# The second norm of a graph and LSTM kernel without back transposes: row factors through DRAM, two scaling passes on VectorE, a rewritten passage and end

## The reference, cut to what matters

```
h = item_feat @ W_item.T + b_item                 # 10000 x 128
b = layernorm(x) @ W_user.T + b_user
x1 = x + relu(adj @ h + b)
z = layernorm(x1) @ W_ih.T + b_ih + b_hh          # input of the LSTM, the "second norm"
i, f, g, o per step: c = sig(f) c + sig(i) tanh(g); hs = sig(o) tanh(c)
g = argmax(hs @ W_lin.T + b_lin)                  # 0 or 1 per row
w = g * hs; inc = cumsum(w); prefix = inc - w; suffix = inc[-1] - inc
out = x1 + 2 hs + prefix * fw_att + suffix * bw_att
```

## Time and profile before

| what | value |
|---|---|
| median of 3 runs | 1447.24 us |
| profiled execution | 1444.94 us, of which the span 1443.1 us |
| granted TensorE clock over the span | 0.993 |
| busy: TensorE, VectorE, ScalarE, GpSimd | 1412.8, 1242.8, 1067.8, 214.5 us |
| HBM read, written | 422.42 MB, 10.28 MB |

### The profile page before, as it was taken

One profiled execution on the slowest core, in us unless ns is written; L12 is line 12 of the kernel. 1 busy time (PEld: TensorE's weight loads), 2 busy tenths in 40 slices (PEclk: granted clock), 3 DMA queues, 4 the chain that ended last, 5 costly groups with the idle time before them and its releaser, 6 DMA issues.

```text
span 1443.1 us, 26187 instructions
## 1 busy us (share of the span) xinstructions
PE 1412.8 (98%) x7478; PEld 1214.0 (84%) x7478; DVE 1242.8 (86%) x2052; ACT 1067.8 (74%) x1502; POOL 214.5 (15%) x193
## 2 busy tenths in 40 slices
PE   8999999999999999999999999999999899999994
PEld 7878888888888888888888888888888799999993
DVE  7998998998998999999989989989989666676667
ACT  6677777777877877877877877777777576556662
POOL 0000010010001001001001001000000132027775
PEclk9999999999999999999999999999999999999997
DMA  9999999999999999999999999999999203000003
GB/s 374 360 331 357 403 364 370 407 360 362 404 365 364 407 357 364 407 355 377 396 358 387 385 352 401 378 347 403 373 362 400 87 0 142 0 2 0 1 0 143
DMA packets 134877, 433.16 MB, mean 300 GB/s; under 512 B 18683, under 2 KB 35900, under 8 KB 134718
## 3 DMA queue, kind: packets, MB, share of 16 engines
q1 hardware_dynamic: 127776, 426.43, 78.0%
q10 hardware_dynamic: 7070, 6.34, 1.6%
HBM read 422.42 MB, written 10.28 MB: 300 GB/s over the span
## 4 chain that ended last, share of the span: by engine, by line
PE 91%; DVE 3%; issue 2%; POOL 2%; DMA 1%; ACT 0%; POOLq 0%; DVEq 0%; SPq 0%; ACTq 0%
PE psG L842 24%; PE psG L843 24%; PE psG L844 24%; PE psZ L965 8%; PE psZ L951 2%; PE psZ L953 2%; PE psZ L955 2%; PE psG L863 1%; PE psT L810 1%; PE psI L890 1%; DVE a_lo L1130 1%; POOL own L526 1%; PE psZ L971 1%; DMA raw<-in_adj_main 1%; POOL own L529 1%
## 5 line engine op out<-in xcount | busy, mean ns | idle before, releaser
L634 ACT ACTIVATE a_hi<-raw 128x1000 fp32r<-128x1000 f32 (+1 forms) x800 | 821.8, 1031 | 244.8 <-PE psG L844 208.4
L1130 DVE TENSOR_TENSOR a_lo<-raw,a_hi 128x1000 fp32r<-128x1000 f32 (+1 forms) x800 | 911.0, 1170 | 74.5 <-ACT a_hi L634 55.2
L842 PE MATMUL psG<-a_hi,item_hi 128*128 128x500 f32 x1560 | 620.5, 398 | 2.1 <-DVE a_lo L1130 1.1
L843 PE MATMUL psG<-a_lo,item_hi 128*128 128x500 f32 x1560 | 606.0, 388 | 0.0
L844 PE MATMUL psG<-a_hi,item_lo 128*128 128x500 f32 x1560 | 604.7, 388 | 0.0
L842 PEld LDWEIGHTS psG<-a_hi,item_hi 128*128 128x128 f32 x1560 | 293.5, 188 | 66.9 <-issue 5.6
L844 PEld LDWEIGHTS psG<-a_hi,item_lo 128*128 128x128 f32 x1560 | 293.2, 188 | 59.4
L843 PEld LDWEIGHTS psG<-a_lo,item_hi 128*128 128x128 f32 x1560 | 293.6, 188 | 58.6 <-issue 4.4
L452 POOL TENSOR_TENSOR rstd<-var,minus_half 125x4 f32<-125x4 f32 x40 | 76.1, 1902 | 1019.5 <-DVE var L1106 1019.5
L965 PE MATMUL psZ<-hist,wh 128*128 (+1 forms) x1264 | 167.8, 276 | 1.2 <-DVE hist L1304 1.1
L965 PEld LDWEIGHTS psZ<-hist,wh 128*128 128x128 f32 x1264 | 154.9, 192 | 1.7 <-issue 1.6
(11 more groups left out here) (174 smaller groups left out, 769.9 us busy)
## 6 DMA issues: line engine op xcount, KB each, us to landing
raw<-in_adj_main SPq DMA_DIRECT2D x760, 500.0 KB, 6.5
raw<-in_adj_main SPq DMA_DIRECT2D x40, 250.0 KB, 4.5
sq<-rstd_copy ACTq DMA_DIRECT2D x20, 250.0 KB, 7.1
x_copy<-xb SPq DMA_DIRECT2D x20, 250.0 KB, 7.1
u<-x_copy SPq DMA_DIRECT2D x1, 5000.0 KB, 14.4
out<-u SPq DMA_DIRECT2D x25, 200.0 KB, 2.4
u<-in_itemT SPq DMA_DIRECT2D x9, 512.0 KB, 10.1
xb<-in_xT SPq DMA_DIRECT2D x18, 250.0 KB, 5.9
```

What stands on the lines that cost most here:

```text
L634: nc.scalar.activation(a_hi[:, s % CUT, 0:n], raw[:, r % RAW, at:at + n], ACT.Copy)\
L842: pe.matmul(bank, w_hi, hi, start=(c == 0), stop=False)
L843: pe.matmul(bank, w_hi, lo, start=False, stop=False)
L1130: last = dve.tensor_tensor(a_lo[:, s % CUT, 0:m], raw[:, r % RAW, at:at + m], a_hi[:, s % CUT, 0:m].bitcast(f32), ALU.subtract)
```

## The change

**Second norm.** `normalise` and `to_columns` are gone. `rstd` and `shift_rows` become the two halves of one tile `row_terms`. ScalarE stores it in DRAM (`send_terms`, r = 8) and reads each half back to all partitions (`spread_terms`, r = 12) into `factors` (which is `sq`) and `rl` (which is `un_bb`). VectorE then multiplies and adds (`apply_rstd`, r = 16; `apply_shift`, r = 17) over 128 x 500, into `normed`. `row_scale` moves from r = 6 to 7, `out_u` from 10 to 18, and reads `normed` in SBUF instead of `psV`. `add_relu` writes a tile of its own, `x1b`, so the load of the next x waits for `x1_ready` alone.

**Passage.** TensorE runs 8 products of `ident` with itself whose result nobody reads (`KEEP_WARM`), then step 1's recurrent part for group a before the back transposes; its step for group b comes after the split inputs of step 2. ScalarE and VectorE take up the cell of step 1 earlier, and `input_hi(1)` moves ahead of step 0's second group.

**End.** GpSimd adds hist and x1 of its last pair before it waits for the gate. ScalarE copies the last two rows of x1 to a tile without strides (`x1_last`) during the LSTM. TensorE adds row L - 2 up before the last logits, and the totals before row L - 1. `total` is computed before the second `last_y`, and ScalarE writes the shift twice, to PSUM for VectorE and to SBUF for GpSimd. There are 13 outputs of 400, 800 or 1000 columns (GpSimd still has 80 chains of 250), and the check stands behind all of them.

```
+OUT_ENDS = (10, 20, 30, 40, 60, 80, 105, 130, 155, 180, 205, 230, K)
+POOL_OUTS = (3, 5, 8, 11)
-AT = dict(... scale2=6, norm2=7, back2=8, out2=10,
+AT = dict(... scale2=7, send2=8, spread2=12, apply2=16, shift2=17, out2=18,
...
-            def normalise(count):
-                act.wait_ge(ln_scale, count)
-                for s in range(SUB):
-                    last = nc.scalar.activation(normed[0:SW, s * HID:(s + 1) * HID], psT[0:SW, s * HID:(s + 1) * HID],
-                                                ACT.Identity, bias=shift_rows[:, s:s + 1], scale=rstd[:, s:s + 1])
-                last.then_inc(ln_normed, 1)
+            def send_terms(j):
+                act.wait_ge(ln_scale, j)
+                act.dma_start(rows_dram.rearrange("k (p s) -> p k s", s=SUB), row_terms[:, :, :])\
+                    .then_inc(terms_stored, 16)
+            def spread_terms(j):
+                act.wait_ge(terms_stored, 16 * j)
+                for k, t in enumerate((factors, rl)):
+                    act.dma_start(t[:, 0:BW], rows_dram[k:k + 1, :].to_broadcast([P, BW])).then_inc(terms_spread, 16)
...
             def out_u(count, odd, pair):
-                act.wait_ge(ln_back, count)
+                act.wait_ge(ln_applied, 2 * count)
...
-            def to_columns(count):
-                pe.wait_ge(ln_normed, count)
-                for s in range(SUB):
-                    last = pe.transpose(psV[:, s * SW:(s + 1) * SW], normed[0:SW, s * HID:(s + 1) * HID],
-                                        ident[0:SW, 0:SW])
-                last.then_inc(ln_back, 1)
...
             def add_relu(j):
                 dve.wait_ge(relu_done, j + 1)
-                dve.tensor_tensor(xb[:, j % 2, :], xb[:, j % 2, :], rl[:, :], ALU.add).then_inc(x1_ready, 1)
+                if not (isinstance(j, int) and j == 0):
+                    dve.wait_ge(x1_stored, 16 * j)
+                dve.tensor_tensor(x1b[:, :], xb[:, j % 2, :], rl[:, :], ALU.add).then_inc(x1_ready, 1)
+            def by_s(t):
+                return t.rearrange("p (s r) -> p s r", s=SUB)
+            def by_r(t):
+                return t.rearrange("p (r s) -> p s r", s=SUB)
+            def apply_rstd(j):
+                dve.wait_ge(terms_spread, 32 * j)
+                if not (isinstance(j, int) and j == 1):
+                    dve.wait_ge(u_ready, j - 1)
+                dve.tensor_tensor(by_s(normed[:, 0:BW]), by_s(x1b[:, :]), by_r(factors[:, :]), ALU.mult)\
+                    .then_inc(ln_applied, 1)
+            def apply_shift(j):
+                dve.wait_ge(ln_applied, 2 * j - 1)
+                dve.tensor_tensor(by_s(normed[:, 0:BW]), by_s(normed[:, 0:BW]), by_r(rl[:, :]), ALU.add)\
+                    .then_inc(ln_applied, 1)
...
             pe.wait_ge(end_relu, 2)
+            for _ in range(KEEP_WARM):
+                pe.matmul(psG[:, 1, 0:P], ident[:, :], ident[:, :], start=True, stop=True)
+            from_state(1, 0, 0, 1)
...
-            def sums(i, par, reset=False):
+            def sums(i, par, reset=False, last=False):
+                if last:
+                    pool.wait_ge(h_ready[0], W + 2 * i + 2)
+                    pool.wait_ge(h_ready[1], W + 2 * i + 2)
+                    pool.wait_ge(y_ready, i - 1)
+                    base(i, par)
                 pool.wait_ge(gated, i + 1)
...
-            pe.wait_ge(t1_ready[0], STEPS)
-            pe.wait_ge(t1_ready[1], STEPS)
+            pe.wait_ge(t1_ready[0], STEPS - 1)
+            pe.wait_ge(t1_ready[1], STEPS - 1)
+            pe.wait_ge(x1_last_ready, 2)
+            add_up(ident, hist[:, L - 2, :], 0, first=True)
+            add_up(ident, x1_last[:, 0, :], 0)
             pe.wait_ge(run_ready, 2 * PAIRS - 1)
-            add_up(ident, hist[:, L - 2, :], 0, first=True)
+            pe.wait_ge(dfd_ready, 1)
+            add_up(dfd, run[:, 1, 0, :], 0, last=True).then_inc(row_sums, 1)
             add_total(run[:, 1, 0, :], first=True)
```

More of the change, by code:

```diff
@@ L524, in sums @@
                     write_y(i - 1, 1 - par)
-                rows = x1[:, :].rearrange("p (k l) -> p l k", l=L)[:, ds(2 * i, 2), :]
-                pool.tensor_tensor(own[:, par, :, :], hist[:, ds(2 * i, 2), :], rows, ALU.add).then_inc(base_ready, 1)
+                if not last:
+                    base(i, par)
                 pool.wait_ge(base_ready, i + 1)
@@ L545, in _ @@
                 sums(2 * i + 1, 1)
-            sums(PAIRS - 2, 0)
+            sums(PAIRS - 2, 0, last=True)
             pool.wait_ge(run_c_ready, PAIRS - 1)
@@ new lines, in first_cell_tanh @@
+            def first_cell_tanh(g):
+                act.wait_ge(c_ready[g], 1)
+                nc.scalar.activation(tb(g, 3), group(C, g), ACT.Tanh, scale=0.5).then_inc(th_ready[g], 1)
+            first_gates(0)
+            first_cell_tanh(0)
+            act.wait_ge(ln_scale, NB)
+            for s in range(2):
+                nc.scalar.activation(normed[0:SW, s * HID:(s + 1) * HID], psT[0:SW, s * HID:(s + 1) * HID],
+                                     ACT.Identity, bias=shift_rows[:, s:s + 1], scale=rstd[:, s:s + 1])\
+                    .then_inc(end_normed_a, 1)
@@ L762, in _ @@
+            act.wait_ge(end_u_v, 1)
+            act.wait_ge(end_u_a, 2)
+            input_hi(1)
+            first_gates(1)
+            cell_tanh(1, 0)
+            first_cell_tanh(1)
+            nc.scalar.activation(slots[:, K - 12:K - 11, HL:L], psT[:, 0:HL].unsqueeze(1), ACT.Copy, bias=1.0)\
+                .then_inc(end_u_a, 1)
             act.wait_ge(special, 2)
             act.wait_ge(dfb_ready, 1)
-            input_hi(1)
-            for r in range(1, 4):
+            gate_pair(1, 1, 0, 1)
@@ L766, in _ @@
+            gate_pair(1, 1, 1, 1)
+            input_hi(2)
+            cell_tanh(1, 1)
+            for r in range(2, 4):
                 lstm(r, r % 2, lambda: input_hi(r + 1))
@@ L778, in _ @@
             lstm_pair(1, 1)
+            act.wait_ge(x1_back, 16)
+            for half in range(2):
+                nc.scalar.activation(x1_last[:, half, :], last_row(x1, L - 2 + half), ACT.Copy).then_inc(x1_last_ready, 1)
             with nc.scalar.Fori(1, PAIRS // 2 - 1) as i:
@@ L1338, in _ @@
                               None, ALU.add).then_inc(end_u_v, 1)
+            forget_product(1, 0)
+            input_product(1, 0)
+            cell(1, 0)
             first_cell(1)
+            state(1, 0, 1)
             state(0, 1, 0)
-            for r in range(1, 4):
+            forget_product(1, 1)
+            input_product(1, 1)
+            cell(1, 1)
+            state(1, 1, 1)
+            for r in range(2, 4):
                 lstm(r, r)
@@ L1412, in _ @@
                 .then_inc(cum_ready, 1)
-            last_y(1)
             dve.wait_ge(cum_ready, 4)
```

293 lines of the change are left out of this document (145 added, 148 removed).

## The result

The changed kernel takes 1440.53 us (median of 7 runs, 1436.9 to 1442.52) where the kernel before takes 1446.77 (7 runs, 1445.31 to 1449.9): a ratio of 0.9948, 95% interval 0.9934 to 0.9962. It is faster, and inside the range given, but by 6.2 us of medians, and by 4.4 us between the two profiled executions (1444.94 and 1440.53), where the sum had 13.5. So the question is where 9 us of the expected gain went.

A forecast was written before the change was run, and what follows sets the result against it. TensorE was taken to bound the kernel (91% of the chain), VectorE close behind in the product. Terms -8.4 + 1.0 - 2.6 - 3.6 + 0.1 = -13.5 us gave 1431.4 from the profiled execution, 1433.7 us as median; range 1429 to 1442.5.

The forecast's parts named there:

- Rival A: In the product, VectorE's lead over TensorE is not enough: 0.5 us lost per block, 1442.2 us; chance 0.15.
- Back transposes, 0.44 us each: In the product, dropping the four transposes in each of 19 blocks frees 0.44 us of TensorE each: 8.4 us gained.
- So the passes fit, by 0.1 to 0.25 us: VectorE's two new passes per block leave `a_lo` just ahead of TensorE, costing 0.05 us per block, 1.0 us in all.
- The walk: Step-by-step count of `a_lo`'s lead over TensorE at a block's end: 0.25 us left at piece 18, 0.23 at piece 19.
- Nothing for SyncE's loads: In the product, the two reads' 0.51 MB delay no loads, since 2.2 us of DMA room at the block's end absorbs 1.2.
- Passage, -2.6: Between product and LSTM: clock losses gone (-2.2 us), group a's part off the path (-0.9), group b's part later (+0.5).
- rival B: In the passage, the clock falls all the same despite the unread products: +2.2 us, 1435.9 us; chance 0.08.
- End, -3.6: After the LSTM, first addition 1.9 us earlier and output written without a hole, ending at 1439.5 us: -3.6 us.
- Rival C: At the end, the check finishes last or writes stay at 382 GB/s: +0.5 to 1.6 us, about 1434.8 us; chance 0.08.
- The two copies, +0.1: In the LSTM, ScalarE's copies of x1's last rows, under 0.6 us each, cost +0.1 us, between 0 and 0.6.
- Rival D: The row terms' store is late and holds ScalarE at piece 12, making the kernel slower: 1475.7 us; chance 0.06.
- in time by 1.8 us: In the product, the row terms' store lands after 9.5 us, before ScalarE's queue needs it at 11.3 us.

The follow-up runs named there:

- run 2: The changed kernel without VectorE's two passes, the DMAs of the row terms kept: 1432.95 us, 0.9899 of the kernel before; block 1 to block 19 takes 986.2 us.
- run 6: The changed kernel with `out_u` reading x1's buffer and waiting only for the two reads, both passes kept: 1439.09 us, 0.9940 of the kernel before.
- Run 1: The changed kernel without the store and the two reads of the row terms, both passes kept: 1442.61 us, 0.9970 of the kernel before.
- run 3: The changed kernel without VectorE's two passes and without the store and reads of the row terms: 1434.73 us, 0.9916 of the kernel before.
- the new order: The changed kernel with the next block's first norm three pieces earlier, its send still at 15, and the passes at pieces 15 and 17: 1438.63 us.
- run 11: The changed kernel without the eight unread products in the passage: 1441.9 us, 0.9949 of the kernel before.
- run 5: The changed kernel with the first norm three pieces earlier, its send at piece 11, and the passes at 15 and 17: 1455.65 us, 1.0056 of the kernel before.
- run 9: The changed kernel with the first norm three pieces earlier, its send kept at piece 15, passes at 15 and 17: 1438.63 us, 0.9930 of the kernel before.
- run 4: The changed kernel with the second norm of the kernel before, new passage and end kept: 1441.53 us, 0.9958 of the kernel before.
- run 10: run 9 with the two copies of x1's last rows moved from ScalarE to GpSimd: 1435.57 us, 0.9913 of the kernel before.
- run 12: run 10 without the store and the two reads of the row terms, passes kept: 1430.59 us, 0.9882 of the kernel before.

## Why the prediction was right, and which of its steps failed

**Right in sign and range, but the likeliest case did not come.** Rival A did, which had a chance of 0.15, at nearly the price it had: 0.5 us per block and 1442.2 us; measured 997.4 - 986.2 = 11.2 us in 18 blocks, 0.62 each, and 1440.53. The median lies in the range because the range was drawn to take in rival A, not because the sum was good: it gave -13.5 us, and the sign rests on passage and end alone.

- **Back transposes, 0.44 us each: right.** 55.23 - 54.79 us in the median block (run 2).
- **"So the passes fit, by 0.1 to 0.25 us ... I put 0.05 us per block": this step failed.** The term was 1.0 us in all; 11.2 us were lost in the stage. The walk itself was good at piece 18: 0.26 us of lead where 0.25 was forecast. At piece 19 it had 0.23, and TensorE stood; two small things are short of the walk: `out_u` begins 0.14 us behind the pass's end (521.75 to 521.89), and it keeps ScalarE for 0.97 us (521.89 to 522.86) instead of 0.89. Of the 0.62 us per block, 0.36 are the fixed stops at piece 19 and at the next block's start. I had treated a lead of 0.1 us as a gain kept in full.
- **The missing half: no feedback to the loads.** The walk took raw pieces as present. `a_lo` also gives the raw buffer back, so VectorE's delay at pieces 16 to 19 moved the load of the next block's piece 2 by 0.9 us nearer to its use and those beside it by less. TensorE's stops at pieces 2 to 5, behind late raw pieces, are the other 0.26 us per block, and run 6 shows that they grow when the first half is taken away. (The kernel before lost some 2.4 us in 18 blocks in the same way, 1.7 of them in block 1, so the stage fell by 10.3 us in run 2, not only by 18 x 0.44 = 7.9.)
- **"Nothing for SyncE's loads": right in the order as changed.** Run 1 puts the cost at 0.3 to 0.9 us in the stage, and runs 2 and 3 find none without the passes, so it was not hidden behind their stops. The loads did land later; what covered it is that they are issued 12.7 us ahead of their products there. In the new order, with 10.9 to 11.4 us, the same traffic costs 4.6 us (990.8 against 986.2). The prediction's argument, room on the DMA engines at the block's end, leaves out how far ahead a load is issued.
- **Passage, -2.6: -2.1 measured.** The clock did not fall, so rival B did not come. Its price of 2.2 us was too high for the unread products alone: run 11, where the clock fell, puts them at 1.26. Which part fell short by 0.5 us is open.
- **End, -3.6: -4.2 measured.** The first addition came 2.0 us earlier against the last recurrent group (forecast 1.9). Rival C did not come: the check took 2.6 us instead of 4.4 and ended at 1434.1, while the last store landed at 1438.3, and the bytes left at 400 GB/s and more.
- **The two copies, +0.1: +0.9 measured,** above the upper end of 0.6. I had priced them as ScalarE time against its idle time summed over a step. They stand together, 1.25 us, in front of a gate that the next step waits for.
- **Rival D, the store late: TensorE lost next to nothing, but "in time by 1.8 us" failed.** The store landed after 11.7 us in the median, not 9.5, and up to 13.0, where the rival put the first cost at 13.3; ScalarE's queue stood for it in 18 of 19 blocks. The roundings behind it had enough lead: TensorE's largest stop there is 0.16 us, in the block with the longest wait. That it cost no more was partly luck, with the latest landing 0.3 us short of the rival's mark. The Trainium skill (DMA: Bandwidth & Descriptors, Specifications) has a read-modify-write below 512 bytes; no run here separates that from the price of the earlier trace rows, which was 2.2 us too low.

Summed: +1.0 - 2.1 + 0.9 - 4.2 = -4.4 us, which is the difference of the two profiled executions.

## What to carry to other kernels

A lead that is walked down to 0.1 or 0.2 us is within the walk's own error, which was 0.2 us here: count it as lost until it has a margin above that. (Above it a lead is kept: 0.28 us at piece 14 of the kernel before cost nothing in any block, 0.25 at piece 18 of the changed kernel next to nothing.) And ask what else the late instruction gives back (here the raw buffer, and with it the next load). When two suspects share one wait, remove each alone and both together, and again after each reordering: the traffic cost 0.9 us at most in one order of the block and 4.6 or more in the other, where the loads are issued less far ahead. Work that is added to an engine with idle time should be placed by the waits of that engine and by what stands in its queue, since one send four pieces earlier cost 17 us (run 5 against run 9), 9.6 of them in block 0.

## What the runs showed of the hardware

- Beside GpSimd, VectorE's subtractions of two SBUF tensors took more than twice as long. The check's first instruction before the change, while GpSimd adds from 1428.17 to 1432.63:

```profile
1429.87 1.06 DVE L1439 TENSOR_TENSOR dif<-hist,cap_h 128x249 f32<-128x249 f32 x1
```

  The same instruction takes 0.42 us at 1431.46 in the changed kernel, where GpSimd has been done since 1429.4. The check's second and third instruction took 1.07 and 1.22 us before and take 0.42 and 0.68 now; its last two, which ran behind GpSimd in both kernels, took 0.42 and 0.67 both times. This is where 1.8 us of the check went, which I had not forecast. VectorE's additions of an SBUF and a PSUM tensor, 128 x 400, took 0.56 us beside GpSimd and without it. The Trainium skill (Advanced Engine Details and Errata, GPSIMD Details) says that the two engines share a read and a write interface and that VectorE's instructions with two SBUF inputs conflict with GpSimd's; the rows agree.
- TensorE's clock fell to its lower level of 1.2 GHz behind an idle time of 2.52 us (run 11), and in run 4 behind two of 1.10 and 0.65 us with one group of eight products between them. In the changed kernel 1.09 and 0.66 us at the same place left it at 1.00. So the length of one idle time does not tell.
- Two DMA reads of 250 KB, each spreading one row over 128 partitions, made the 500 KB loads beside them land after 8.0 instead of 5.4 us (block 8 of runs 10 and 12).
- A store of 250 runs of 16 bytes, issued while SyncE's loads keep the DMA engines full, landed after 11.7 us in the median and 13.0 at most.
